# LoRA's second factor in 64 rows per output tile, two output tiles at once in the two halves of the array; outputs finished in pairs

## What is computed

```
result = einsum('bsd,od->bso', x, base_weight) + base_bias
A, Bw  = lora_A_w[ids], lora_B_w[ids]
h      = einsum('bsd,brd->bsr', x, A)          # rank 16
result = result + einsum('bsr,bor->bso', h, Bw)
query  = result @ Wq.T ; u = gelu(result @ Wu1.T + bu1) @ Wu2.T ...
out    = x + result + gate * (attention over 512 slots @ Wvd.T @ Wvu.T)
```

## Time and profile before

| | |
|---|---|
| median of 3 runs | 1922.83 us (1919.9 to 1925.39) |
| profiled execution, its own time | 1922.93 us |
| its span, first to last instruction | 1921.1 us |
| TensorE matmuls | 8464, busy 1903.1 us (99%) |
| VectorE busy | 1276.5 us (66%) |
| ScalarE busy | 704.9 us (37%) |
| SyncE issues of `b_raw` | 192, 32.0 KB each, median 369 ns of SyncE |
| one operation on `ax` (32 x 512) | ScalarE 587 ns, VectorE 680 ns |
| granted TensorE clock, mean | 0.999 of full |

### The profile page before, as it was taken

One profiled execution on the slowest core, in us unless ns is written; L12 is line 12 of the kernel. 1 busy time (PEld: TensorE's weight loads), 2 busy tenths in 40 slices (PEclk: granted clock), 3 DMA queues, 4 the chain that ended last, 5 costly groups with the idle time before them and its releaser, 6 DMA issues.

```text
span 1921.1 us, 24555 instructions
## 1 busy us (share of the span) xinstructions
PE 1903.1 (99%) x8464; PEld 1549.0 (81%) x8464; DVE 1276.5 (66%) x1668; ACT 704.9 (37%) x1115; POOL 396.7 (21%) x275
## 2 busy tenths in 40 slices
PE   8999999999999999999999999999999999999998
PEld 6888888888888888888888877777878888888887
DVE  5796688565468746447874743677666677676576
ACT  4332334333233333224333322345444233233333
POOL 2210222020022202002211100220443322323332
PEclk9999999999999999999999999999999999999999
DMA  7878667451466744146754435666978777777797
GB/s 274 300 283 290 214 235 233 152 181 59 149 204 233 242 141 171 55 156 227 236 202 143 165 103 184 224 203 227 323 258 266 246 240 236 243 236 249 230 358 298
DMA packets 196784, 416.54 MB, mean 217 GB/s; under 512 B 26868, under 2 KB 28404, under 8 KB 196534
## 3 DMA queue, kind: packets, MB, share of 16 engines
q1 hardware_dynamic: 151158, 325.83, 51.4%
q10 hardware_dynamic: 45504, 89.15, 12.1%
HBM read 317.37 MB, written 97.52 MB: 216 GB/s over the span
## 4 chain that ended last, share of the span: by engine, by line
PE 89%; issue 4%; DVE 4%; ACT 1%; POOL 1%; DMA 1%; ACTq 0%; DVEq 0%; SPq 0%; POOLq 0%
PE bank L1896 19%; PE bank L1897 19%; PE bank L1898 19%; PE bank L1935 6%; PE bank L1936 6%; PE bank L1937 6%; PE bank L2055 1%; PE bank L2057 1%; PE bank L2056 1%; PE bank L1827 1%; PE bank L1839 1%; PE bank L1840 1%; PE bank L1953 1%; PE bank L1952 1%; PE bank L2020 1%
## 5 line engine op out<-in xcount | busy, mean ns | idle before, releaser
L1896 PE MATMUL bank<-xop,wsp 128*128 128x512 f32 x1792 | 707.8, 395 | 6.9 <-DVE wsp L1331 6.0
L1897 PE MATMUL bank<-xop,wsp 128*128 128x512 f32 x1792 | 700.0, 391 | 0.0
L1898 PE MATMUL bank<-xop,wsp 128*128 128x512 f32 x1792 | 699.1, 390 | 0.0
L1896 PEld LDWEIGHTS bank<-xop,wsp 128*128 128x128 f32 x1792 | 337.3, 188 | 89.4 <-DVE wsp L1331 6.0
L1897 PEld LDWEIGHTS bank<-xop,wsp 128*128 128x128 f32 x1792 | 337.5, 188 | 74.2 <-issue 3.8
L1898 PEld LDWEIGHTS bank<-xop,wsp 128*128 128x128 f32 x1792 | 337.0, 188 | 71.8
L909 ACT ACTIVATE wsp<-wraw 128x1024 fp32r<-128x1024 f32 x184 | 195.0, 1060 | 510.6 <-PE bank L1898 503.5
L1331 DVE TENSOR_TENSOR wsp<-wraw,wsp 128x1024 fp32r<-128x1024 f32 x184 | 232.4, 1263 | 161.0 <-ACT wsp L909 160.3
L891 POOL TENSOR_TENSOR r_h<-r_h,r_x 128x512 f32<-128x512 f32 x128 | 174.4, 1363 | 362.2 <-DMA r_h<-h_dram 327.4
L1935 PE MATMUL bank<-h_sp,wu 128*128 128x512 f32 x512 | 201.0, 393 | 1.4 <-DVE stage L1422 1.4
L1936 PE MATMUL bank<-h_sp,wu 128*128 128x512 f32 x512 | 200.2, 391 | 0.0
(11 more groups left out here) (180 smaller groups left out, 1923.8 us busy)
## 6 DMA issues: line engine op xcount, KB each, us to landing
xraw<-in_x SPq DMA_DIRECT2D x248, 256.0 KB, 4.1
wraw<-in_w SPq DMA_DIRECT2D x115, 512.0 KB, 3.8
wraw<-t_dram SPq DMA_DIRECT2D x88, 512.0 KB, 3.5
h_dram<-stage ACTq DMA_DIRECT2D x128, 256.0 KB, 2.6
hraw<-h_dram SPq DMA_DIRECT2D x128, 256.0 KB, 4.1
r_x<-in_x SPq DMA_DIRECT2D x128, 256.0 KB, 4.3
r_h<-h_dram SPq DMA_DIRECT2D x128, 256.0 KB, 3.5
out<-o_st ACTq DMA_DIRECT2D x96, 256.0 KB, 3.8
```

What stands on the lines that cost most here:

```text
L1896: pe.matmul(ps, wsp[:, slot, 0, f], x_hi(i), start=(k == 0), stop=False)
L1897: pe.matmul(ps, wsp[:, slot, 0, f], x_lo(i), start=False, stop=False)
L1898: last = pe.matmul(ps, wsp[:, slot, 1, f], x_hi(i), start=False, stop=(k == HT - 1))
```

## The change

The LoRA product of one output tile now takes 64 rows in place of 96: four groups of 16 rows hold low(A)x, high(A)x, the low rest of high(A)x, and high(A)x again, and face high, high, high and low parts of the second factor. The same 64 rows are repeated on partitions 64 to 127. An even output tile's second factor lies on partitions 0 to 63, the odd one's on 64 to 127. `lora_b(g-2)` and `lora_b(g-1)` are issued one behind the other in every second tile, in the two halves of rows of the array and into two banks. So `finish` runs for two tiles in a row in every second turn, `add_sums` one tile later than before, and two `square_and_store` every second turn.

Around it: `load_b` issues eight DMAs of 16 rows x 2 x 128 in place of six of 16 x 512; `split_a` is six ScalarE and two VectorE operations in place of three and three; `b_sp` is one operation of 128 x 256 on each engine; new masks, made once in turn 1, choose which rows get the low part; the second batch's first factor goes into the bank of the statistics (`xa_ps`) and its preparation (`ax2_hi`, `ax2_lo`) becomes a chain of ScalarE copy, VectorE addition, ScalarE, VectorE, ScalarE. The matmuls of `lora_a_step` are as many as before; those of M1 are 128 columns wide now.

```diff
-KL = 6 * RANK
+KL = 4 * RANK
@@ split of the first factor
-                to_hi(a_sp[:, :, 0, 0:RANK], a_raw[:, 0, :, :])
-                to_hi(a_sp[:, 0:HT, 1, 0:RANK], a_raw[:, 1, 0:HT, :])
-                to_hi(a_sp[:, :, 3, 0:RANK], a_raw[:, 1, :, :]).then_inc(ah_ready, 1)
+                for i in range(2):
+                    for j in range(1, 4):
+                        last = to_hi(a_sp[:, :, i, j * RANK:(j + 1) * RANK], a_raw[:, i, :, :])
+                last.then_inc(ah_ready, 1)
@@ ScalarE, squares and stores
-                if g > 1 and tile_of(g - 2)[1] in H_PRODUCTS:
+                if g > 2 and tile_of(g - 3)[1] in H_PRODUCTS and g % 2 == 1:
+                    square_and_store(g - 3)
                     square_and_store(g - 2)
@@ SyncE
-                for r in range(6):
-                    sp.dma_start(b_raw[r * RANK:(r + 1) * RANK, :], lora_b[which, c]).then_inc(b_in, 16)
+                for r in range(8):
+                    half = lora_b[which, c].rearrange("r (i e f) -> r e i f", i=2, e=2)[:, r // 4, :, :]
+                    sp.dma_start(b_raw[r * RANK:(r + 1) * RANK, :, :], half).then_inc(b_in, 16)
@@ VectorE, end of a turn and end of the first stage
-                if g > 1 and tile_of(g - 2)[1] in H_PRODUCTS:
-                    add_sums(g - 2)
-                if g > 0 and tile_of(g - 1)[1] in H_PRODUCTS:
+                if g > 2 and tile_of(g - 3)[1] in H_PRODUCTS:
+                    add_sums(g - 3)
+                if g > 1 and tile_of(g - 2)[1] in H_PRODUCTS and g % 2 == 0:
+                    finish(g - 2)
                     finish(g - 1)
...
+            finish(TILES - 2)
             finish(TILES - 1)
+            add_sums(TILES - 3)
+            split_wu_lo(7)
             add_sums(TILES - 2)
-            split_wu_lo(7)
             add_sums(TILES - 1)
@@ VectorE, second batch's first factor
-                dve.wait_ge(ax2h_ready, p + 1)
-                lo(ax2[0:32, :], lora_ps[32:64, :], ax2[32:64, :]).then_inc(ax2_ready, 1)
+                dve.wait_ge(lora2_done, p + 1)
+                dve.wait_ge(axh_ready, 3 * p + 2)
+                dve.tensor_tensor(xa_raw[0:KL, :], xa_ps, xa_raw[0:KL, :], ADD).then_inc(axl_ready, 1)
+                dve.wait_ge(axh_ready, 3 * p + 3)
+                dve.wait_ge(axl_ready, 3 * p + 2)
+                dve.scalar_tensor_tensor(ax2[0:KL, :], xa_raw[0:KL, :], low_x[0:KL, :], ax2[0:KL, :].bitcast(f32), MULT, ADD)\
+                    .then_inc(axl_ready, 1)
@@ TensorE
-                pe.matmul(main_ps[g % NBANK][:], b_sp[:, chunk % 2, (o % 4) * P:(o % 4 + 1) * P], ax[:],
+                rows = slice(o % 2 * KL, (o % 2 + 1) * KL)
+                pe.matmul(main_ps[g % NBANK][:], b_sp[rows, chunk % 2, o % 4 // 2, :], ax[rows, :],
                           start=False, stop=True, skip_group_check=True).then_inc(lb_done, 1)
...
-                    if k == 5 and g > 0 and tile_of(g - 1)[1] in H_PRODUCTS:
+                    if k == 5 and g > 1 and tile_of(g - 2)[1] in H_PRODUCTS and g % 2 == 0:
+                        lora_b(g - 2)
                         lora_b(g - 1)
...
+            lora_b(TILES - 2)
             lora_b(TILES - 1)
```

More of the change, by code:

```diff
@@ L157, in bass_adaln_ffn @@
         part = sb("part", [P, 2 * TT * GROUPS])
+        masks = sb("masks", [P, 4])
+        low_b, low_x, sign_b, sign_x = (masks[:, i:i + 1] for i in range(4))
         xop = at(at_xop, "xop", [P, NX, 2, S], f32r)
@@ L169, in bass_adaln_ffn @@
         t4_raw = sums[:, 0, :, :].rearrange("p a s -> p (a s)")
-        a_sp = at(at_asp, "a_sp", [P, KT, 4, 2 * RANK], f32r)
+        a_sp = at(at_asp, "a_sp", [P, KT, 2, KL], f32r)
         a_raw = at(at_lora, "a_raw", [P, 2, KT, RANK])
[L172 to L175, removed]
+        b_raw = at(at_lora + 2 * K, "b_raw", [P, 2, P])
+        xa_raw = at(at_lora + 6 * K, "xa_raw", [P, S])
+        b_sp = at(at_lora + 4 * K, "b_sp", [P, 2, 2, P], f32r)
+        ax1 = at(at_lora + 8 * K, "ax1", [P, S], f32r)
+        ax2 = at(at_lora + 10 * K, "ax2", [P, S], f32r)
         v_sp = at(at_t, "v_sp", [P, 2, TT, VB], f32r)
@@ L224, in bass_adaln_ffn @@
         stat_ps = stat_bank[:, 0:2 * TT * GROUPS]
+        xa_ps = stat_bank[0:KL, :]
         u_ps = bank[0:4]
@@ L268, in bass_adaln_ffn @@
         lora2_done = sem("lora2_done")
-        ax1h_ready = sem("ax1h_ready")
+        masks_ready = sem("masks_ready")
+        axh_ready = sem("axh_ready")
+        axl_ready = sem("axl_ready")
         ax1_ready = sem("ax1_ready")
-        ax2h_ready = sem("ax2h_ready")
         ax2_ready = sem("ax2_ready")
@@ L946, in split_a_hi @@
                 wait(act, lora2_done, p)
-                to_hi(a_sp[:, :, 0, 0:RANK], a_raw[:, 0, :, :])
-                to_hi(a_sp[:, 0:HT, 1, 0:RANK], a_raw[:, 1, 0:HT, :])
-                to_hi(a_sp[:, :, 3, 0:RANK], a_raw[:, 1, :, :]).then_inc(ah_ready, 1)
+                for i in range(2):
+                    for j in range(1, 4):
+                        last = to_hi(a_sp[:, :, i, j * RANK:(j + 1) * RANK], a_raw[:, i, :, :])
+                last.then_inc(ah_ready, 1)
             def split_b_hi(p, j):
-                act.wait_ge(b_in, 6 * 16 * (8 * p + j + 1))
+                act.wait_ge(b_in, 8 * 16 * (8 * p + j + 1))
+                act.wait_ge(masks_ready, 5)
                 wait(act, lb_done, (8 * p + j - 1) * 4)
-                to_hi(b_sp[:, j % 2, :], b_raw[:]).then_inc(bh_ready, 1)
+                act.activation(b_sp[:, j % 2, :, :], b_raw[:], ACT.Copy, scale=sign_b[:]).then_inc(bh_ready, 1)
             def split_x_hi(p, q, k):
@@ L983, in ax1_hi @@
                 wait(act, lb_done, 4 * HT * p)
-                act.activation(ax1[0:32, :], lora_ps[0:32, :], ACT.Copy)
-                act.activation(ax1[64:96, :], lora_ps[0:32, :], ACT.Copy).then_inc(ax1h_ready, 1)
+                act.activation(ax1[0:KL, :], lora_ps[0:KL, :], ACT.Copy, scale=sign_x[0:KL, :]).then_inc(axh_ready, 1)
+                act.activation(xa_raw[0:KL, :], lora_ps[KL:P, :], ACT.Copy).then_inc(axh_ready, 1)
+                act.wait_ge(axl_ready, 3 * p + 1)
+                act.activation(ax1[KL:P, :], ax1[0:KL, :].bitcast(f32), ACT.Copy).then_inc(ax1_ready, 1)
             def ax2_hi(p):
-                act.wait_ge(lora2_done, p + 1)
-                act.activation(ax2[32:64, :], lora_ps[32:64, :], ACT.Copy)
-                act.activation(ax2[64:96, :], lora_ps[32:64, :], ACT.Copy).then_inc(ax2h_ready, 1)
+                act.wait_ge(axl_ready, 3 * p + 2)
+                act.activation(ax2[0:KL, :], xa_raw[0:KL, :], ACT.Copy, scale=sign_x[0:KL, :]).then_inc(axh_ready, 1)
+                act.wait_ge(axl_ready, 3 * p + 3)
+                act.activation(ax2[KL:P, :], ax2[0:KL, :].bitcast(f32), ACT.Copy).then_inc(ax2_ready, 1)
             def square_and_store(g):
@@ L1361, in split_a_lo @@
                 dve.wait_ge(ah_ready, p + 1)
-                lo(a_sp[:, :, 0, RANK:], a_raw[:, 0, :, :], a_sp[:, :, 0, 0:RANK])
-                lo(a_sp[:, 0:HT, 1, RANK:], a_raw[:, 1, 0:HT, :], a_sp[:, 0:HT, 1, 0:RANK])
-                lo(a_sp[:, :, 3, RANK:], a_raw[:, 1, :, :], a_sp[:, :, 3, 0:RANK]).then_inc(al_ready, 1)
+                for i in range(2):
+                    last = lo(a_sp[:, :, i, 0:RANK], a_raw[:, i, :, :], a_sp[:, :, i, RANK:2 * RANK])
+                last.then_inc(al_ready, 1)
             def split_b_lo(p, j):
                 dve.wait_ge(bh_ready, 8 * p + j + 1)
-                lo(b_sp[64:KL, j % 2, :], b_raw[64:KL, :], b_sp[64:KL, j % 2, :]).then_inc(bl_ready, 1)
+                b = b_sp[:, j % 2, :, :].rearrange("p i f -> p (i f)")
+                dve.scalar_tensor_tensor(b, b_raw[:].rearrange("p i f -> p (i f)"), low_b[:], b.bitcast(f32), MULT, ADD)\
+                    .then_inc(bl_ready, 1)
             def split_x_lo(p, q, k):
@@ L1376, in ax1_lo @@
             def ax1_lo(p):
-                dve.wait_ge(ax1h_ready, p + 1)
-                lo(ax1[32:64, :], lora_ps[0:32, :], ax1[0:32, :]).then_inc(ax1_ready, 1)
+                dve.wait_ge(axh_ready, 3 * p + 1)
+                dve.scalar_tensor_tensor(ax1[0:KL, :], lora_ps[0:KL, :], low_x[0:KL, :], ax1[0:KL, :].bitcast(f32), MULT, ADD)\
+                    .then_inc(axl_ready, 1)
             def ax2_lo(p):
-                dve.wait_ge(ax2h_ready, p + 1)
-                lo(ax2[0:32, :], lora_ps[32:64, :], ax2[32:64, :]).then_inc(ax2_ready, 1)
+                dve.wait_ge(lora2_done, p + 1)
[4 more added lines that the diff above has]
+                dve.scalar_tensor_tensor(ax2[0:KL, :], xa_raw[0:KL, :], low_x[0:KL, :], ax2[0:KL, :].bitcast(f32), MULT, ADD)\
+                    .then_inc(axl_ready, 1)
             def combine(g):
@@ L1438, in add_sums, with make_masks @@
                     dve.tensor_tensor(into, into, stage[:, n % NST, :, :], ADD).then_inc(sum_ready, 1)
+            def make_masks():
+                odd = ident[:].rearrange("p (a b j) -> p a b j", a=2, b=2)
```

(23 more changed lines are left out.)

3 lines of the change are left out of this document (1 added, 2 removed).

## The result

The changed kernel takes 1936.77 us, median of five runs (1934.58 to 1939.36), against 1924.67 us for the kernel before in the same comparison; the ratio is 1.0078 (95% interval 1.0065 to 1.0091), so it is slower by 0.8%. The forecast was 1937.9 us, or before + 15.0.

The account below looks back on a forecast made before the run. The prediction took an almost unbroken queue of TensorE matmuls to bound the kernel. Its terms, 13.8 + 0.8 - 0.9 + 1.3 = +15.0 us on 1922.9, gave 1937.9 us, with an 8-in-10 range of 1923 to 1948 us.

Parts of the forecast that it names:

- The array: TensorE at lora_b: 64-row matmuls wait going in and out, as at router_keys, whose total was 0.32 us.
- D: Rival at the lora_b pairs: no empty array needed, loads go ahead, halves overlap; -15.0 us, 1907.9 us; chance 0.13.
- The price of a pair: Two lora_b on TensorE: 0.721 us against 0.506 before, 0.215 more, times 64 makes +13.8 us.
- The loads: Two more DMA issues per chunk on SyncE, 64 in all, some 0.4 us each: nothing, weights being three tiles ahead.
- The banks: Later finish of the even tile: hidden, over 6 us against 1.5 us for two finish, unless VectorE is over 4 behind.
- The first M6 tile: TensorE's 0.90 us wait for xop: add_sums moves behind these operands, so -0.9 us; bound 0.
- Start: Kernel start, where TensorE already waits 0.59 us: split_a on ScalarE goes from 3 operations to 6, +0.8 us.
- Turn: Turn to the second stage: two squares in a row about +0.6, one more add_sums +0.7; together +1.3 us, bound 0 to 2.5.
- The other edits: Longer ax2 chain has two tiles, about 11 us, until its first lora_b; smaller b_sp and turn 1 masks: all nothing.
- B: Rival at the lora_b pairs: in and out paid, halves run one after the other; +22.6, 1945.5 us; chance 0.17.
- E: Rival at the lora_b pairs: no switch and no overlap, or the two cancel; +1.2, 1924.1 us; chance 0.10.
- C: Rival at the lora_b pairs: switch costs only the router's total, both loads hidden in it; 1926.7 us; chance 0.10.

Follow-up runs that it names:

- full height: Changed kernel with every lora_b over all 128 rows in place of one half, nothing else changed: 1924.81 us, ratio 1.0021 to the kernel before.
- the pair issued twice: Changed kernel with the two lora_b of each pair issued twice in a row: 1952.6 us, ratio 1.016 to the kernel before.
- pairs-only kernel: Kernel before with lora_b, finish and squares in pairs and add_sums one tile later; 96 rows, six loads, old preparation kept: 1922.21 us, ratio 1.0004.
- each half alone: Changed kernel in the order of before, each 64-row lora_b alone in its own tile: 1971.67 us, ratio 1.0264 to the kernel before.

## Why the prediction was right

It was right in direction, and the array's part in it was right for the reason given. That the size came out so close, 1937.9 us against 1936.8, is in part luck: errors of several us offset each other.

- **The array.** The core of the argument was that a form of 64 rows isn't loaded ahead, on the way in nor out, read from two odd matmuls of the router. The prediction says that no other matmul does what `router_keys` does; `router_factor`, with 48 rows, does it too in the same trace: the matmul before it starts at 1290.39, the load of `router_factor` at 1290.70, the next full load at 1291.70. The reading held in every pair (0.32 us from the start of the matmul before to the load, 0.43 in the one pair at the half clock), and full height alone takes the wait away (0.23 us from the matmul before to the first of the pair, whose load starts with the matmul before). It is paid once per change of form, not per matmul, as the pair issued twice shows (1.32 against 1.09 us). What the load waits for, an empty array as D puts it or something else, no run shows.
- **The price of a pair.** 0.721 us was forecast, 0.66 measured, so 9.6 us in place of 13.8. The term that was too large is "0.107 by which the odd half starts later, because its load follows on the same path": it is 0.004, and the two loads of a pair together take 0.18 us, as long as one, against 0.29 on the same rows. My lower bound, 0.614 without offset, was nearer: 1.09 less two matmuls of 0.227 is 0.634, as 0.09 wait on entry, 0.107 load, 0.227 stream, 0.10 wait on the way out and 0.11 for the exposed full load; the last 0.02 lie on the matmuls behind, as with the 96-row form. The loads that D has going ahead did not: from the full form into a half they start 0.32 us behind the matmul before, not with it.
- **The loads.** "Two more DMA issues per chunk on SyncE ... Both nothing" is the step that failed. I counted the issues at the 0.37 us of the old shape and looked at the weights queued behind them, not at ScalarE and VectorE, which wait for these very loads in their own order. With the waits for a bank (2.6), the longer wait for xop (2.0) and the half clock behind it (1.5) that was most of some 6.9 us.
- **The banks.** "Hidden; it would take VectorE being over 4 us behind" failed in the first pair of batches, where tiles 12, 14 and 16 waited 2.1 us for a bank. The deferred `add_sums`, which was to help there, did not prevent it; behind the first pair of batches no such wait is left, as forecast.
- **The first M6 tile.** For the same reason the 0.9 us gain didn't come. In the pairs-only kernel it didn't come either, with a wait of 1.4 us: the deferred `add_sums` did not help there.
- **Start and turn.** Start: 0.8 forecast, 0.45 measured, by one trace each; tile 1 of the versions with this start lies between 0.2 us before and 2.4 us after the 18.69 of before, so the term isn't measured well. Turn: +1.3 forecast; between tile 223 and the ninth step the difference moved by -0.1. TensorE's wait for `stage` ahead of the second stage vanished, and the wait for h_sp grew from 0.58 to 1.23. The longer wait for h_sp comes with the order: pairs only has it too, 1.4. The one for `stage` is 0.3 in pairs only and is missing in each half alone, which has the order of before but a later TensorE; which of the two ended it here stays open.
- **The other edits** (the longer chain for `ax2`, masks) show nothing, as forecast: no wait of TensorE is put down to them, in the changed kernel or at full height.
- **The sum.** 9.6 + 6.9 + 0.45 - 0.1 = 16.9 us against the profiled execution of before, which had its own 2.6 us of bad luck in the second stage, and the spans are 13.6 apart; the medians are 12.1 apart, and the interval of the ratio says 12.5 to 17.5. Against the forecast's terms the pairs were 4.2 us less and the turn 1.4 less, the start 0.35 less, and the loads with the first M6 tile 7.8 us more.
- **The rivals.** B falls with the halves 4 ns apart, D and E with the held-back loads, C with 0.66 us.

## What to carry to other kernels

Before a small matmul is put into half the array to save another, look in the trace for any matmul of that height among full ones, and read from start to start on both sides of it: here a switch cost 0.43 us beside the one stream (0.66 less 0.23), so it must save about two matmuls before it pays, not one. When a load's shape changes, look up what one issue costs in the new shape (0.56 us here, 0.37 in the old one) and who waits for it in order, not only what is queued behind it. An order that is free by itself, as the pairing was, can still cost when another engine comes late (2.1 us of waits for a bank in the changed kernel, none of them with the loads issued earlier). And a matmul of 96 rows was not cheaper here than one of 128 (0.253 us against 0.227).

## What the runs showed of the hardware

- A 96-row matmul among full ones costs 0.253 us, the same padded to 128 rows 0.227; the 0.026 lie in the starts of the matmuls behind it.
- Two 64-row matmuls on the same rows start 0.335 us apart, on different rows 0.004. The 0.335 are, added up, the first one's exposed load, 0.107, and one stream of 0.227; the second's load runs meanwhile, although its rows are the same. A second pair behind a first one likewise starts 0.335 behind it, and adds 0.23 in all: the 0.107 are paid once, by the first.
- A lone 64-row matmul among full ones costs as much as a pair in two halves: 1.08 against 1.09 us from the matmul before to the second full one behind.
- One DMA issue on SyncE takes 369 ns for 16 rows in one piece (of 2 KB or 1 KB) and 562 ns in two pieces of 512 bytes, though it moves 16 KB, half of the 32 KB in pieces of 2 KB.
- Some 1.4 us after the end of an idle stretch of 2.8 us, with matmuls running again, the granted clock fell to 0.50 of full for 3.4 us; full matmuls then started 0.43 us apart in place of 0.23.
